# Query and key projections of one attention stage as two halves of 256 columns instead of one matmul of 512

## The chip, the cores and the metric

The kernel runs on one core of one Trainium2 chip. The metric is the device time of one execution in microseconds (us). Three runs of the kernel before gave 2101.59 us as their median, from 2100.45 to 2105.27.

## What is computed

Four blocks follow one another on an activation x of 16 batches x 128 rows x 256 features, with a context of the same shape: a channel attention (stage 0), a transformer layer with self and cross attention (stage 1), a latent attention (stage 2) and a block with two wide cross attentions and an MLP (stage 3). Only stage 3 is touched. Cut to what matters, in the reference it is

```python
D, H, K, F = (256, 16, 128, 1024)
def _cross_attention(q_in, kv_in, wq, bq, wk, bk, wv, bv, wo, bo, bias_k, bias_v):
    qh = (q_in @ wq + bq).reshape(b, q_len, H, K)
    kh = (kv_in @ wk + bk).reshape(b, t, H, K)
    vh = (kv_in @ wv + bv).reshape(b, t, H, K)
    kh = jnp.concatenate([kh, bias_k ...]); vh = jnp.concatenate([vh, bias_v ...])
    weights = softmax(einsum('bqhk,bthk->bhqt', qh, kh) / scale)
    return einsum('bhqt,bthk->bqhk', weights, vh).reshape(b, q_len, H * K) @ wo + bo
x = x + _cross_attention(_layer_norm(x, ...), xf_1, ...)
x = x + _cross_attention(_layer_norm(x, ...), xf_2, ...)
x = x + gelu(_layer_norm(x, ...) @ w_fc1 + b_fc1) @ w_fc2 + b_fc2
```

Both contexts are the same array. There are 16 heads of 128 columns, over 16 x 128 rows of x and of the context.

## The kernel before, in words

Stage 3 works through two attention layers (a = 0, 1), each as 8 pairs of heads. All rows, 16 batches x 128 = 2048, are cut in G = 4 quarters of R = 512 rows. A pair has STEPS = 8 steps, t = 0 to 7: one for each head and quarter. In every step TensorE (PE) makes, in this order: the scores of this step into a score bank (L1997, plain fp32, 8 recorded matmuls of 128 columns), the weighting of the values of the step before into o_psum (L2015, again 8), then the step's share of the projections and output products, and last the 4 transposes of the probabilities (L2074). The projections are one step or more ahead of their use; their order is the list in `pair_work` (L1204), and they go through four PSUM banks of 512 columns named `general`, taken in turn.

All products of projections and outputs use split numbers: each operand is held as a high part and a low part in the format fp32r, and `split_matmul` (L1949) adds three products (high x high, low x high, high x low) for each of the KC = 2 chunks of 128 features, thus six matmuls for each result. Each of the six has its own stationary operand, so that each matmul comes with one weight load.

- `queries` (L1972) and `keys` (L1978) fill one bank with one result of 128 rows x 512 columns: stationary is a 128x128 piece of w_qk, moving are 512 rows of hT (the normalised x, transposed) or of ctxT (the context, transposed). Six matmuls of 512 columns.
- `values` (L1983) and `output` (L2018) fill a bank with two results of 256 columns, one after the other: 12 matmuls of 256 columns. Stationary is ctxT or oT, moving is w_v or w_o.

In a whole pair there are 8 query and 8 key projections (96 matmuls of 512 columns), 8 banks of values and 8 of outputs (192 matmuls of 256 columns), 64 score matmuls, 64 for the weighting and 32 transposes. The pairs are: a `lead` pair written out, six pairs in a hardware loop (`pe.Fori(1, PAIRS - 1)`, L2139 and L2156), and a last one written out (`turn` after the first layer, `end` after the second). The lead pair has no values to make, since these were made before it.

The steps of a looped pair hold, after the 8 + 8 matmuls of scores and weighting: steps 1 and 2 two projections and two banks of values; step 3 one projection and two banks of values; step 4 three projections alone; steps 5 and 6 two projections and two banks of outputs; step 7 two projections and one bank of outputs. Step 0 has two projections and two banks of values right behind the last outputs of the pair before, which in the trace stand as a string of 24 matmuls of 256 columns, with the wait for the low part of oT inside it.

What runs beside: ScalarE (ACT) takes queries out of PSUM (L1622), makes the exponentials (L1629) and copies the transposed probabilities (L1637) and the weighted values (L1645); VectorE (DVE) takes out keys (L1768) and values, the maximum of the scores (L1782) and adds outputs to x (L1806); GpSimd (POOL) divides the probabilities by their sums (L1533) and subtracts high parts for low parts, of hT at L1502. Each general bank has a count `full` and a count `free`; a projection waits for `free` before its first matmul, and its last matmul raises `full`. `next_queries` (L2098) makes the queries of head 0 of a layer's first pair and waits for the low part of hT (`hT_ready`) inside the projection, ahead of the two matmuls that read it (`wait_low`, L1956).

Three key projections of the first pair are made in stage 2 by other code (L1160), and the MLP's up product has its own function (L2107).

Of the kernel before, what the change touches and what calls it, by code (L numbers as in the profile page):

```python
# [26 lines left out]
P = 128  # L27
B = 16
D = 256
KC = D // P  # L30
NB = 4
G = B // NB
R = NB * P
# [1292 lines left out]
def stage_3(nc, dram, consts, early):  # L1326

    ident, cols = consts["ident"], consts["cols"]

    with ExitStack() as ctx:  # L1330
        def sb(name, shape, dt=F32):
            return ctx.enter_context(nc.sbuf_tensor(name, shape, dt))
# [9 lines left out]
        rows = sb("rows3", [P, len(ROWS_B), D])  # L1342
# [12 lines left out]
        kT, ctxT, raw_qk, raw_v, raw_vrows = [early[name] for name in ("kT", "ctxT", "raw_qk", "raw_v", "raw_vrows")]  # L1355
        w_qk, w_v, vrow, hcols = [early[name] for name in ("w_qk", "w_v", "vrow", "hcols")]
        mv, rstd, shift = early["mv"], early["rstd"], early["shift"]
        hT = sb("hT3", [P, 2, KC, B * P], F32R)
# [40 lines left out]
        def wait_free(eng, *at):  # L1399

            k, n = bank_count(*at)
            eng.wait_ge(free[k], n + 1)
            return general[k], full[k]
# [26 lines left out]
        def quarter(g):  # L1430
            return slice(g * R, (g + 1) * R)
# [10 lines left out]
        with nc.Block() as block:  # L1442
# [503 lines left out]
            def _(pe):  # L1946
                seed(pe, [s["scores_ready"], s["pT_ready"], s["o_ready"]] + full)

                def split_matmul(out, stationary, moving, low_last=None, wait_low=None):  # L1949


                    terms = [(a, b, c) for c in range(KC) for a, b in PASSES]
                    if low_last is not None:
                        terms.sort(key=lambda term: term[low_last] == LO)
                    for i, (a, b, c) in enumerate(terms):
                        if wait_low is not None and i == 2 * KC:  # L1956
                            wait_low()
                        last = nc.tensor.matmul(out, stationary(a, c), moving(b, c), start=(i == 0), stop=(i == len(terms) - 1))  # L1958
                    return last

                def transposed(section, a, g):
                    for c in range(KC):
# [6 lines left out]
                            last = nc.tensor.transpose(out[:, b * P:(b + 1) * P], xhat(g, b)[:, c * P:(c + 1) * P], ident[:, :])  # L1969
                        last.then_inc(filled, 1)  # L1970

                def queries(section, a, i, key, head, wait_low=None):  # L1972
                    out, filled = wait_free(pe, section, a, i, key)
                    t = key[1]
                    split_matmul(out[:, :], lambda part, c: w_qk[:, head, part, c * P:(c + 1) * P],
                                 lambda part, c: hT[:, part, c, quarter(t % G)], 1, wait_low).then_inc(filled, 1)

                def keys(section, a, i, t, head):  # L1978
                    out, filled = wait_free(pe, section, a, i, ("k", t))
                    split_matmul(out[:, :], lambda part, c: w_qk[:, head, part, (KC + c) * P:(KC + c + 1) * P],  # L1980
                                 lambda part, c: ctxT[:, part, c, quarter(t % G)]).then_inc(filled, 1)

                def values(section, a, i, key):  # L1983

# [46 lines left out]
                def pair(a, i, kind):  # L2031
                    section, loop = kind, i if kind == "pair" else 0
                    weights = a * PAIRS + i + 2
                    for t in range(STEPS):
# [22 lines left out]
                        for key in pair_work(kind)[t]:  # L2057
                            if key[0] == "q":
                                queries(section, a, loop, key, 1 - key[1] // G)
                            elif key[0] == "late":  # L2060
                                next_queries(section, a, key)
                            elif key[0] == "k":
                                keys(section, a, loop, key[1], 1 - key[1] // G)
                            elif key[0] == "v":
                                values(section, a, loop, key)
                            else:
                                if key[2] == 0:
                                    pe.wait_ge(s["o_hi"], n + 1)
                                output(section, a, loop, key[1], key[2], (lambda: pe.wait_ge(s["o_lo"], n + 1)) if key[2] == 0 else None)
# [28 lines left out]
                def next_queries(section, a, key):  # L2098

                    pe.wait_ge(s["hT_hi"], a * G + key[1] % G + 2)  # L2100
                    queries(section, a, 0, key, 0, lambda: pe.wait_ge(s["hT_ready"], a * G + key[1] % G + 2))
# [18 lines left out]
                def down(g, f, b):  # L2120
                    if f == 0 and g > 0:
                        pe.wait_ge(s["down_added"], (g - 1) * NB + b + 1)
                    for k, (up_part, down_part) in enumerate(PASSES):
                        last = nc.tensor.matmul(down_sums[b][:, 0:D], upT[:, up_part, f, b * P:(b + 1) * P], w_down[:, down_part, f, :],  # L2124
                                                start=(f == 0 and k == 0), stop=(f == FC - 1 and k == len(PASSES) - 1))
                    return last

                keys("open", 0, 0, 7, 0)
                next_values("open", 2)
                transposed("open", 0, 0)  # L2130
# [36 lines left out]
                for g in range(G - 1):  # L2167

                    for f in range(FC):
                        up(g + 1, (f,))  # L2170
                        wait_upT(g, f)
                        for b in range(NB):
                            last = down(g, f, b)
                        last.then_inc(s["down_read"], 1)
                for b in range(NB):
                    for f in range(FC):
                        if b == 0:
                            wait_upT(G - 1, f)
                        last = down(G - 1, f, b)
# [103 lines left out]
```

## Time and profile before

| | |
|---|---|
| median of three runs | 2101.59 us (2100.45 to 2105.27) |
| profiled execution, its span | 2100.9 us |
| what lies around the span in the profiled execution | not shown on its own; the median of the runs is 0.7 us above the span |
| TensorE busy | 1933.4 us, 92% of the span |
| weight loads busy (overlap with the matmuls) | 1680.5 us |
| VectorE, ScalarE, GpSimd busy | 1277.2, 1184.1, 678.0 us |
| matmuls recorded | 14880, with as many weight loads |
| of them projections of queries and keys by `queries` and `keys` | 768 + 750, of 512 columns |
| stage 3 | from about 950 us to the end |

How to read it: a matmul's recorded duration holds the way through the array, so that it overlaps with the next one's. The pace of a row of matmuls is the time from the start of its first one to the start of what comes next, divided by their number, and not the duration of one. The timeline merges neighbours of one kind in one row, with the start of the first and the time until the end of the last.

### The profile page before, as it was taken

Reading aid. Unit: us, or ns where it says so; the run is one execution under the profiler, and the core shown is the slowest. Engines: PE = TensorE matmul, PEld = TensorE weight load, DVE = VectorE, ACT = ScalarE, POOL = GpSimd, SP = SyncE. Lnnn points to the kernel's source line nnn. Section 1 sums busy time; section 2 is a strip of 40 time slices with the busy share of each in tenths; the row PEclk is TensorE's granted clock in tenths of the full one; section 3 lists DMA queues with packets and bytes.
Section 4 is the critical chain, followed back from the end, with each engine's and each line's share of the span. In section 5 each row is a group of like instructions: output and inputs, shape, how many; then the busy total and the mean of one; then the engine's idle time right before and its main releaser. Section 6 shows DMA issues by size and latency. Waiting matters only on the chain.

```text
span 2100.9 us, 43190 instructions
## 1 busy us (share of the span) xinstructions
PE 1933.4 (92%) x14880; PEld 1680.5 (80%) x14880; DVE 1277.2 (61%) x4143; ACT 1184.1 (56%) x3878; POOL 678.0 (32%) x613
## 2 busy tenths in 40 slices
PE   4578899999999899888999999999899999999889
PEld 3457678787778777676999999999799999999778
DVE  2577797979797865445555555556455555555663
ACT  2466888778787876546444444443644444444531
POOL 1233443434444343533222221223312222223452
PEclk8889999999999999999999999999999999999999
DMA  7000000000000000001000000000000000000100
GB/s 262 6 11 7 6 7 7 12 2 7 2 7 2 3 2 2 22 1 43 26 16 25 25 20 15 25 15 26 11 26 21 20 25 20 15 20 0 41 11 31
DMA packets 24635, 44.35 MB, mean 21 GB/s; under 512 B 2336, under 2 KB 12064, under 8 KB 23584
## 3 DMA queue, kind: packets, MB, share of 16 engines
q1 hardware_dynamic: 23328, 34.13, 5.2%
q10 hardware_dynamic: 1152, 8.26, 1.0%
q8 instruction: 85, 1.39, 0.3%
q14 instruction: 70, 0.57, 0.1%
HBM read 40.28 MB, written 2.10 MB: 20 GB/s over the span
## 4 chain that ended last, share of the span: by engine, by line
PE 48%; DVE 2%; ACT 2%; issue 1%; POOL 1%; ACTq 0%; DVEq 0%; POOLq 0%
PE general L1958 32%; PE o_psum L2015 6%; PE scores L1997 5%; PE pT_psum L2074 3%; PE scores L2124 1%; ACT probs L1629 1%; POOL probs L1533 1%; PE o_psum L2124 1%; PE pT_psum L2124 1%; ACT oT L1645 0%; DVE oT L1800 0%; PE general L1969 0%; DVE guess L1310 0%; DVE var L1308 0%; DVE row_stats L1762 0%
## 5 line engine op out<-in xcount | busy, mean ns | idle before, releaser
L557 POOL TENSOR_TENSOR probs<-probs,rsums 128x512 f32<-128x512 f32 (+1 forms) x288 | 283.9, 998 | 485.8 <-DVE rsums L787 485.2
L1533 POOL TENSOR_TENSOR probs<-probs,rsums 128x512 f32<-128x512 f32 x128 | 133.4, 1042 | 733.0 <-DVE rsums L1793 733.0
L610 ACT ACTIVATE probs<-negated,negmax 128x128 f32<-128x128 f32 (+1 forms) x768 | 325.5, 431 | 12.1 <-DVE negmax L778 11.9
L1637 ACT COPY probsT<-pT_psum 128x512 f32<-128x512 f32 x128 | 75.0, 586 | 282.6 <-PE pT_psum L2074 282.6
L1105 PE MATMUL pT_psum<-ident,probs 128*128 128x128 f32 x1072 | 174.9, 284 | 53.9 <-ACT probsT L618 26.4
L1105 PEld LDWEIGHTS pT_psum<-ident,probs 128*128 128x128 f32 x1072 | 124.4, 144 | 108.2 <-issue 63.2
L1958 PE MATMUL general<-hT,w_qk 128*128 128x512 f32 x768 | 206.3, 404 | 1.9 <-ACT kT L1612 1.5
L1958 PE MATMUL general<-w_o,oT 128*128 128x256 f32 x1536 | 197.4, 282 | 1.6 <-ACT oT L1645 0.9
L1958 PE MATMUL general<-ctxT,w_qk 128*128 128x512 f32 x750 | 194.1, 394 | 2.9 <-DVEq L222 2.9
L1958 PEld LDWEIGHTS general<-w_o,oT 128*128 128x128 f32 x1536 | 187.8, 188 | 11.3 <-DVE oT L1800 3.8
L1629 ACT ACTIVATE probs<-scores,negmax 128x128 f32<-128x128 f32 x512 | 180.5, 370 | 24.0 <-DVE negmax L1785 24.0
L1645 ACT ACTIVATE oT<-o_psum,hcols 128x512 fp32r<-128x512 f32 x128 | 88.1, 688 | 183.5 <-PE o_psum L2015 183.5
L1958 PEld LDWEIGHTS general<-w_v,ctxT 128*128 128x128 f32 x1488 | 180.0, 189 | 4.5
L1958 PE MATMUL general<-w_v,ctxT 128*128 128x256 f32 x1488 | 182.1, 279 | 0.0
L1800 DVE SCALAR_TENSOR_TENSOR oT<-o_psum,hcols,oT 128x512 fp32r<-128x512 f32 x128 | 96.1, 751 | 119.1 <-ACT oT L1645 119.1
L1958 PEld LDWEIGHTS general<-ctxT,w_qk 128*128 128x128 f32 x750 | 139.4, 188 | 32.7 <-DVEq L222 3.3
L793 DVE COPY probsT<-pT_psum 128x512 f32<-128x512 f32 (+1 forms) x140 | 91.3, 652 | 116.6 <-PE pT_psum L1105 116.3
L1958 PEld LDWEIGHTS general<-hT,w_qk 128*128 128x128 f32 x768 | 136.2, 189 | 26.5 <-issue 2.1
L967 PE MATMUL general<-hT_y,weights_a 128*128 128x256 f32 x640 | 151.6, 383 | 2.6 <-ACT upT L683 1.5
L618 ACT COPY probsT<-pT_psum 128x512 f32<-128x512 f32 (+1 forms) x144 | 80.4, 558 | 126.7 <-PE pT_psum L1105 123.9
L610 ACT ACTIVATION_READ_ACCUMULATOR probs<-negated,negmax 128x1 f32 x768 | 148.7, 194 | 0.0
L2015 PE MATMUL o_psum<-probsT,ctxT 128*128 128x128 f32 x1024 | 141.4, 281 | 1.4 <-ACT probsT L1637 1.4
(198 smaller groups left out, 3922.7 us busy)
## 6 DMA issues: line engine op xcount, KB each, us to landing
raw_qk<-w_qk_dram SPq DMA_DIRECT2D x32, 256.0 KB, 2.8
weights_a<-weights_a_dram ACTq DMA_DIRECT2D x2, 2048.0 KB, 17.8
raw_v<-w_v_dram SPq DMA_DIRECT2D x16, 256.0 KB, 2.7
raw_vrows<-vrows_dram SPq DMA_DIRECT2D x16, 256.0 KB, 3.3
raw_o<-w_o_dram SPq DMA_DIRECT2D x16, 256.0 KB, 2.6
weights_a<-weights_a_dram ACTq DMA_DIRECT2D x3, 1024.0 KB, 10.4
X<-x_dram SPq DMA_DIRECT2D x8, 256.0 KB, 7.3
ctx_in<-ctx_dram SPq DMA_DIRECT2D x8, 256.0 KB, 2.8
```

What stands on the lines that cost most here:

```text
L557: nc.gpsimd.tensor_tensor(pr, pr, rsums[:, n % 4, 0:segs].unsqueeze(2).broadcast_to([P, segs, width(kind) // segs]), ALU.mult).then_inc(s[ ...
L610: last = nc.scalar.activation(probs[:, n % PROBS, i * wide:(i + 1) * wide], src[:, i * wide:(i + 1) * wide], ACT.Exp, scale=1.0 if kind == ...
L793: nc.vector.tensor_copy(probsT[:, n % 4, 0:width(kind)], turned(kind, g, u)[:, 0:width(kind)]).then_inc(s["pT_copied_dve"], 1)
L967: last = nc.tensor.matmul(out[:, j * RA:(j + 1) * RA], w[weight][:, c, chunk * P:(chunk + 1) * P], rhs(c), start=(c == 0), stop=(c == KC - 1))
L1105: last = nc.tensor.transpose(turned(kind, g, u)[:, j * P:(j + 1) * P], probs[:, n % PROBS, j * P:(j + 1) * P], ident[:, :])
L1533: nc.gpsimd.tensor_tensor(pr, pr, rsums[:, t % 2, :].unsqueeze(2).broadcast_to([P, NB, P]), ALU.mult).then_inc(s["probs_ready"], 1)
L1629: nc.scalar.activation(probs[:, t % 2, b * P:(b + 1) * P], scores[t % 2][:, b * P:(b + 1) * P], ACT.Exp, bias=negmax[:, t % 2, b:b + 1], s ...
L1645: nc.scalar.activation(oT[:, HI, head, quarter(t % G)], o_psum[:, :], ACT.Identity, bias=hcols[:, bass.ds(at, 1)]).then_inc(s["o_hi"], 1)
L1800: nc.vector.scalar_tensor_tensor(out=oT[:, LO, head, quarter(t % G)], in0=o_psum[:, :], scalar=hcols[:, bass.ds(at, 1)], in1=oT[:, HI, hea ...
L1958: last = nc.tensor.matmul(out, stationary(a, c), moving(b, c), start=(i == 0), stop=(i == len(terms) - 1))
L1997: last = nc.tensor.matmul(scores[t % 2][:, j * P:(j + 1) * P], qT[:, head, b * P:(b + 1) * P], kT[:, head, b * P:(b + 1) * P], start=True, ...
L2015: last = nc.tensor.matmul(o_psum[:, j * P:(j + 1) * P], v[:, head, (t % G) * NB + j, :], probsT[:, j * P:(j + 1) * P], start=True, stop=True)
```

## The change

`queries` and `keys` fill their bank in two halves: first all six matmuls on columns 0 to 255, then all six on columns 256 to 511. Each half loads its six stationary operands anew. Each result is the same sum in the same order. The count `full` is raised by the last matmul of the second half. The wait for the low part of hT stands in the first half, behind its first four matmuls.

```diff
+                def halves_matmul(out, stationary, moving, at, low_last=None, wait_low=None):
+                    for half in range(2):
+                        cols = slice(half * R // 2, (half + 1) * R // 2)
+                        rows = slice(at + half * R // 2, at + (half + 1) * R // 2)
+                        last = split_matmul(out[:, cols], stationary, lambda part, c: moving(part, c, rows), low_last, wait_low if half == 0 else None)
+                    return last
+
                 def queries(section, a, i, key, head, wait_low=None):
                     out, filled = wait_free(pe, section, a, i, key)
                     t = key[1]
-                    split_matmul(out[:, :], lambda part, c: w_qk[:, head, part, c * P:(c + 1) * P],
-                                 lambda part, c: hT[:, part, c, quarter(t % G)], 1, wait_low).then_inc(filled, 1)
+                    halves_matmul(out, lambda part, c: w_qk[:, head, part, c * P:(c + 1) * P],
+                                  lambda part, c, rows: hT[:, part, c, rows], t % G * R, 1, wait_low).then_inc(filled, 1)
 
                 def keys(section, a, i, t, head):
                     out, filled = wait_free(pe, section, a, i, ("k", t))
-                    split_matmul(out[:, :], lambda part, c: w_qk[:, head, part, (KC + c) * P:(KC + c + 1) * P],
-                                 lambda part, c: ctxT[:, part, c, quarter(t % G)]).then_inc(filled, 1)
+                    halves_matmul(out, lambda part, c: w_qk[:, head, part, (KC + c) * P:(KC + c + 1) * P],
+                                  lambda part, c, rows: ctxT[:, part, c, rows], t % G * R).then_inc(filled, 1)
```

## Rows read from the trace of the kernel before

**Rows 1.** The page, part 1: busy time, share of the span, instructions.

```profile
PE 1933.4 (92%) x14880; PEld 1680.5 (80%) x14880; DVE 1277.2 (61%) x4143; ACT 1184.1 (56%) x3878; POOL 678.0 (32%) x613
```

**Rows 2.** Stretches: length, busy PE, PEld, DVE, ACT, POOL, then PEclk; second: one pair.

```profile
1090.00:1404.00 314.00, 313.82 (x2236) 290.59 (x2235) 163.93 (x319) 145.77 (x500) 70.40 (x65) 1.00 0.07 21
...
1152.90:1215.87 62.97, 62.92 (x451) 58.24 (x450) 32.99 (x65) 29.15 (x100) 14.08 (x13) 1.00 0.07 21
```

**Rows 3.** Chain of waits from 1216 to 1280 us, by line.

```profile
by line: PE general L1958 70.5%; PE o_psum L2015 11.9%; PE scores L1997 9.8%; PE pT_psum L2074 5.5%; DVE oT L1800 1.2%; ACT oT L1645 1.1%; issue 0.3%; ACTq L1644 0.0%
```

**Rows 4.** The page, part 5: TensorE's groups of projections, values and outputs.

```profile
L1958 PE MATMUL general<-hT,w_qk 128*128 128x512 f32 x768 | 206.3, 404 | 1.9 <-ACT kT L1612 1.5
L1958 PE MATMUL general<-w_o,oT 128*128 128x256 f32 x1536 | 197.4, 282 | 1.6 <-ACT oT L1645 0.9
L1958 PE MATMUL general<-ctxT,w_qk 128*128 128x512 f32 x750 | 194.1, 394 | 2.9 <-DVEq L222 2.9
...
L1958 PE MATMUL general<-w_v,ctxT 128*128 128x256 f32 x1488 | 182.1, 279 | 0.0
```

**Rows 5.** Timeline of PE, steps 0, 4 and 5: start, us to last end.

```profile
1217.78 1.54 PE L1958 MATMUL general<-hT,w_qk 128*128 128x512 f32 x6
...
1220.53 2.91 PE L1958 MATMUL general<-w_v,ctxT 128*128 128x256 f32 x24
1223.28 0.60 PE L2074 MATMUL pT_psum<-ident,probs 128*128 128x128 f32 x4
...
1247.59 1.63 PE L1958 MATMUL general<-ctxT,w_qk 128*128 128x512 f32 x6
1249.06 1.54 PE L1958 MATMUL general<-hT,w_qk 128*128 128x512 f32 x6
...
1251.81 0.60 PE L2074 MATMUL pT_psum<-ident,probs 128*128 128x128 f32 x4
...
1254.01 1.62 PE L1958 MATMUL general<-hT,w_qk 128*128 128x512 f32 x6
...
1256.84 2.91 PE L1958 MATMUL general<-w_o,oT 128*128 128x256 f32 x24
1259.59 0.60 PE L2074 MATMUL pT_psum<-ident,probs 128*128 128x128 f32 x4
```

**Rows 6.** Timeline of PE, the 96 matmuls of 256 columns after the first layer.

```profile
1462.55 3.07 PE L1958 MATMUL general<-w_v,ctxT 128*128 128x256 f32 x24
1465.46 2.99 PE L1958 MATMUL general<-w_o,oT 128*128 128x256 f32 x24
1468.29 5.82 PE L1958 MATMUL general<-w_v,ctxT 128*128 128x256 f32 x48
```

**Rows 7.** Timeline of PE in the last pair; third row: the first's tail alone.

```profile
1942.51 2.98 PE L1958 MATMUL general<-w_v,ctxT 128*128 128x256 f32 x24
1945.33 1.54 PE L1958 MATMUL general<-ctxT,w_qk 128*128 128x512 f32 x6
...
1942.84 2.54 PE L1958 MATMUL general<-w_v,ctxT 128*128 128x256 f32 x21
```

**Rows 8.** Timeline of PE, two of the 14 output banks behind transposes.

```profile
1211.17 1.66 PE L1958 MATMUL general<-w_o,oT 128*128 128x256 f32 x12
...
1606.26 1.62 PE L1958 MATMUL general<-w_o,oT 128*128 128x256 f32 x12
```

**Rows 9.** Waits of PE over the whole span, its row for L2074.

```profile
PE pT_psum L2074 <- POOL probs L1533: 12.0, 10, 2.5
```

**Rows 10.** Timeline of PE, the first query projection and what follows.

```profile
959.86 0.73 PE L1958 MATMUL general<-hT,w_qk 128*128 128x512 f32 x2 [0.32 <-POOL hT L1502]
...
963.35 0.66 PE L1969 MATMUL general<-ident,xhat 128*128 128x128 f32 x4 [1.80 <-DVE ctxT L1775]
```

**Rows 11.** The page: the instruction queue (part 3), a load's landing (part 6).

```profile
q8 instruction: 85, 1.39, 0.3%
...
raw_o<-w_o_dram SPq DMA_DIRECT2D x16, 256.0 KB, 2.6
```

## The prediction

> **What bounds the kernel now.** First the page's busy times: PE is busy for 92% of the span [rows 1]. A share over the span says nothing of one stage, so next the stretches: in five pairs of the loop PE is busy for 313.82 of 314.00 us at the full clock of 2.4 GHz (granted 1.00), while VectorE has 163.93 us of work and ScalarE 145.77 [rows 2]. The chain of waits agrees: from 1216 to 1280 us 70.5% of it is L1958, where projections, values and outputs are multiplied, and nearly all the rest is PE as well [rows 3]. So what a change adds to PE's row of matmuls in the loops comes out in the time one for one, and the other engines' idle time takes nothing of it up.
>
> **What is cut.** 768 + 750 matmuls of 512 columns [rows 4] are 253 projections of six. They become 3036 of 256 columns, with as many weight loads: 1518 matmuls and 1518 loads more, 16398 recorded of each kind instead of 14880. No transfer, copy or count is added, and a bank is full when its second half is. So all hangs on whether two matmuls of 256 take longer than one of 512.
>
> **The tempting reading is wrong.** The groups give 400.4 us for 1518 matmuls of 512, 264 ns each, and 379.5 us for 3024 of 256, 125.5 ns each [rows 4]; two halves would take 251 ns and the change save 13 ns x 1518 = 20 us. But these busy times count the way through the array (394 ns recorded for a matmul of 512) once more at each change of group, and this is spread over 6 matmuls in a projection and over 12 or 24 in values. Starts are what counts. From 1249.06 to 1251.81 us 12 matmuls of 512 take 2.75 us, 229 ns each; from 1256.84 to 1259.59 us 24 of 256 take the same 2.75 us, 114.6 ns each, 229 ns for two [rows 5]. Here halving costs nothing: the price goes by columns, and the weight load of each half is hidden, as it already is in the values and outputs.
>
> The rows thus show no fixed part per matmul. The Trainium skill (TensorE: Matmul & The Clock Gate, "Back-to-back issue gap") has one, N / 2.4 + 2.5 ns: by that rule each of 1518 cut matmuls costs 2.5 ns more, and the sum would be about 4 us higher than at equal prices. The rows at 229 ns and 2 x 114.6 ns contradict it for these operands, and they decide.
>
> **But 256 columns have two paces.** In the string of 96 after the first layer 24 matmuls take 2.83 us (1465.46 to 1468.29 us), 118 ns each, and the 48 behind them keep to it: 5.82 less one duration of 0.28, by 47 gaps, is 118 ns [rows 6]. In the last pair 24 such matmuls take 2.82 us with their start, and the last 21 of them (2.54 - 0.28) / 20 = 113 ns each [rows 7]. Both are alone on PE, both begin right behind the weighting of values, both at full clock. A string keeps its pace to its end: the 96 never leave 118 ns. The 14 output banks that stand alone behind a transpose show how often each comes: 9 take 1.66 us and 5 take 1.62, which over ten gaps is the same 4 to 5 ns [rows 8]. Of the four undisturbed strings that begin with 256 columns behind the weighting, the one of rows 6 is slow and the three of the last pair (those at 1936, 1942 and 1949 us; [rows 7] is the second) are fast. Together 10 of 18 are slow.
>
> Before, a step behind the weighting begins with 512 columns; the values or outputs that follow come out at 2.75 us for 24 [rows 5], close to the fast pace. After, every step is one unbroken string of 256 columns from its first projection on. So the change makes the whole step, also its values and outputs, fall to the one or the other pace.
>
> **The sum, for one looped pair.** A string of n halves takes, slow, 2.91 us for its first 24 (1462.55 to 1465.46) and 0.118 for each more [rows 6]; fast, 2.82 for its first 24 and 0.113 for each more [rows 7].
> - Four steps (1, 2, 5, 6) have two projections and 24 matmuls of 256. Now 1254.01 to 1259.59 = 5.58 us [rows 5]. After, 48 halves: fast 2.82 + 2.71 = 5.53 (-0.05), slow 2.91 + 2.83 = 5.74 (+0.16).
> - Three steps (3, 4, 7) have the work of 36 halves; step 4 stands for them: 1247.59 to 1251.81 = 4.22 us [rows 5]. After: fast 2.82 + 1.36 = 4.18 (-0.04), slow 2.91 + 1.42 = 4.33 (+0.11).
> - Step 0 runs on behind the last outputs: 1217.78 to 1223.28 = 5.50 us [rows 5] for 48 halves' work. Fast 48 x 0.113 = 5.42 (-0.08), slow 48 x 0.118 = 5.66 (+0.16).
> All fast: -0.20 - 0.12 - 0.08 = -0.40 us a pair. All slow: +0.64 + 0.33 + 0.16 = +1.13.
>
> How many pairs: 253 / 16 = 15.8. Off the path are projections in steps where PE waits for the divided probabilities anyway: 10 such waits, 12.0 us together, at L2074 [rows 9], with two or three projections ahead of each, and the three before the first step. Some 27 go, 226 stay, 14 pairs. Bounds: 14 x -0.40 = **-5.6 us** and 14 x 1.13 = **+15.8 us**. I take half the strings at 118 ns, between the 10 of 18 over all and the 1 of 4 behind the weighting: +5.1 us.
>
> **Small things, at nothing.** The wait for hT's low part now stands behind four short matmuls instead of four long ones, with eight short ones (0.92 us) behind it instead of two long (0.46). It binds once, for 0.32 us at 959.86; the 0.46 us more are covered by the wait of 1.80 us that follows at 963.35 [rows 10]; without it they would count. Banks are filled at the same moments within 0.2 us, and the engines that empty them are half idle.
>
> Against the profiled span: 2100.9 + 5.1 = 2106.0 us. The median of the runs lies 0.7 above that span: **2107 us**.
>
> **The rivals.**
> 1. *Mixed paces*, the forecast: 35 to 80% of the strings at 118 ns, +2 to +11.5 us; chance 0.49.
> 2. *113 ns prevails* (the other side: not slower). If the start behind the weighting nearly always leads to 113 ns, as in three of four, the change takes out the slower beginning of the 512s and gives -5.6 to about +1 us, 2096 to 2103. It is decided by the share of strings at 118 ns: the time stays within 0.2% (4.2 us, about what a measurement tells from no change) below a share of (4.2 + 5.6) / 21.4 = 0.46, and is faster by over 0.2% only below 0.07. For it: rows 7. Against it: rows 6 and 8. Chance 0.27.
> 3. *Nearly all at 118 ns*, as the 96 in a row: +11.5 to +15.8, 2113 to 2117. Chance 0.14.
> 4. *The loop's code no longer stays on the core.* One pair has 451 matmuls and 450 loads in the trace [rows 2]. 29760 of both are recorded [rows 1], of which ten repeats of the loops are 9010; the other 20750 against 1.39 MB on the instruction queue are 67 bytes each [rows 11]. Were each repeat fetched again, the queue would carry about 2.0 MB. So a body of 60 KB is kept now; after, with 192 more, it is 73 KB. No row shows whether that much is kept. If not, each of ten jumps back waits for a fetch; the nearest row is a load that lands after 2.6 us [rows 11]: up to 26 us, 2127 with equal paces, or nothing if PE's queue covers it. Chance 0.06. The Trainium skill (Runtime: NRT & Kernel Launch, "Instruction fetch mechanics") gives PE 128 KiB, which would hold 73 KB, but says as well that a jump back beyond two blocks of 16 KiB stalls; the second is not what the 1.39 MB show, since the body is nearly four such blocks already.
> 5. *The busy times were right*: 13 ns saved each, -17 us on 14 pairs, 2084. Only the group means speak for it; the starts speak against. Chance 0.04.
> That the change does not do what it says would show in the count; the diff leaves no case out.
>
> **How the numbers follow.** Faster by over 0.2%: all of 5 and a fifth of 2, 0.09. Slower by over 0.2%: two thirds of 1, all of 3 and 4, 0.53. Within: 0.38. The range runs from nearly all fast, 2097, to all slow, 2117, and leaves out 4, 5 and the edge of 2. The likeliest case's own range is 2104 to 2113.
>
> **What would show it.** 16398 matmuls and loads, none of 512 columns in the projections; PE still busy all through the loops at 1.00; strings of 36 and 48 halves at 4.18 or 4.33 and 5.53 or 5.74 us, in about equal numbers; one looped pair of 63.3 to 63.6 us instead of 62.97 [rows 2]. The forecast is wrong if nearly all strings have one pace, if a third pace appears (the first halves of a bank above 118 ns would be loads that are not hidden), if gaps appear at the loop's ends, or if the instruction queue carries far more than 1.39 MB and the 0.07 MB of new code.

## The result and the profile after

Over 16 runs of each, the changed kernel takes 2109.1 us in the median (2106.85 to 2117.46) and the kernel before 2103.51 us (2099.47 to 2110.7). The ratio is 1.003, with a 95% interval of 1.002 to 1.0039: slower by 5.6 us or 0.27%, with an interval clear of 1. The profiled execution has a span of 2107.1 us against 2100.9.

The page after, span, busy times and TensorE's groups; they answer to [rows 1] and [rows 4]:

```profile
span 2107.1 us, 46226 instructions
PE 1942.2 (92%) x16398; PEld 1757.1 (83%) x16398; DVE 1277.1 (61%) x4143; ACT 1182.9 (56%) x3878; POOL 677.3 (32%) x613
...
q8 instruction: 89, 1.46, 0.3%
...
L1958 PE MATMUL general<-hT,w_qk 128*128 128x256 f32 x1536 | 208.8, 284 | 2.3 <-ACT kT L1612 1.5
L1958 PE MATMUL general<-ctxT,w_qk 128*128 128x256 f32 x1500 | 197.1, 280 | 2.9 <-DVEq L222 2.9
L1958 PE MATMUL general<-w_o,oT 128*128 128x256 f32 x1536 | 197.8, 282 | 1.7 <-ACT oT L1645 0.9
...
L1958 PE MATMUL general<-w_v,ctxT 128*128 128x256 f32 x1488 | 183.6, 280 | 0.0
```

The counts are the forecast ones: 16398 matmuls and as many loads, none of 512 columns in these groups. The other engines' work is unchanged. The four groups' busy times together grow from 779.9 to 787.3 us, +7.4; the values, which the change does not touch, have 1.5 of that. The instruction queue carries 89 packets instead of 85.

Where the 6.2 us of the spans lie. The stages ahead of the change vary from one execution to the next: the first query projection starts at 958.47 us in the profile before and at 957.35 after, 1.1 us earlier. So stage 3, from there to the end, takes 2107.1 - 957.35 = 1149.75 us instead of 2100.9 - 958.47 = 1142.43, which is 7.3 us more. The timeline of PE at the start of stage 3, after, answers to [rows 10]:

```profile
957.35 0.62 PE L1958 MATMUL general<-hT,w_qk 128*128 128x256 f32 x4
958.75 1.21 PE L1958 MATMUL general<-hT,w_qk 128*128 128x256 f32 x8 [0.78 <-POOL hT L1502]
...
962.26 0.66 PE L1969 MATMUL general<-ident,xhat 128*128 128x128 f32 x4 [1.82 <-DVE ctxT L1775]
```

The wait for the low part of hT is 0.78 us instead of 0.32, since four short matmuls now stand ahead of it. The wait of 1.8 us behind the next transposes is still there. From the first query projection to the transposes behind that wait it is 4.91 us (957.35 to 962.26), and it was 4.88 (958.47 to 963.35).

The loops, by stretches (length, then busy PE, PEld, DVE, ACT, POOL, then the granted clock), after; the first and second row answer to [rows 2]:

```profile
1090.00:1404.00 314.00, 313.79 (x2693) 311.61 (x2692) 162.73 (x317) 144.83 (x499) 70.26 (x65) 1.00 0.07 21
1153.40:1216.98 63.58, 63.53 (x547) 63.02 (x546) 32.94 (x65) 29.10 (x100) 14.06 (x13) 1.00 0.07 21
1216.98:1280.60 63.62, 63.57 (x547) 63.05 (x546) 33.03 (x65) 29.10 (x100) 14.05 (x13) 1.00 0.06 21
```

PE has no gap and the full clock, as before, and a pair takes 63.6 us instead of 63.0. From one jump back to the next the ten looped pairs took 62.97 to 63.09 us in the first layer and 63.26 to 63.44 in the second before, and 63.49 to 63.62 and 63.79 to 63.95 after: 0.6 us more for a pair in each layer, 5.9 us over the ten. Lead and last pairs and the start of the stage give the other 1.4.

Inside a pair, the timeline of PE after, steps with 48 halves (first and second) and one with 36 (third); they answer to [rows 5]:

```profile
1163.03 1.66 PE L1958 MATMUL general<-hT,w_qk 128*128 128x256 f32 x12
1164.53 1.58 PE L1958 MATMUL general<-ctxT,w_qk 128*128 128x256 f32 x12
1165.94 2.90 PE L1958 MATMUL general<-w_v,ctxT 128*128 128x256 f32 x24
1168.68 0.60 PE L2083 MATMUL pT_psum<-ident,probs 128*128 128x128 f32 x4
...
1170.87 1.66 PE L1958 MATMUL general<-hT,w_qk 128*128 128x256 f32 x12
1172.37 1.57 PE L1958 MATMUL general<-ctxT,w_qk 128*128 128x256 f32 x12
1173.78 2.99 PE L1958 MATMUL general<-w_v,ctxT 128*128 128x256 f32 x24
1176.60 0.60 PE L2083 MATMUL pT_psum<-ident,probs 128*128 128x128 f32 x4
...
1185.38 1.66 PE L1958 MATMUL general<-ctxT,w_qk 128*128 128x256 f32 x12
1186.87 1.58 PE L1958 MATMUL general<-hT,w_qk 128*128 128x256 f32 x12
1188.29 1.58 PE L1958 MATMUL general<-ctxT,w_qk 128*128 128x256 f32 x12
1189.70 0.60 PE L2083 MATMUL pT_psum<-ident,probs 128*128 128x128 f32 x4
```

Read the starts. In both of the first two steps the keys take 1.41 us for 12, 118 ns each, so the projections are at the slow pace. Then the steps part: the values of the first take 2.74 us for 24 (114 ns each), those of the second 2.82 (117.5). The steps take 5.65 and 5.73 us, where 5.58 stood before. The step of 36 halves is at the slow pace to its end, 4.32 us instead of 4.22.

For a count over the whole of stage 3, all gaps between neighbouring starts in unbroken rows of matmuls of 256 columns at L1958 (950 to 2000 us) were sorted to the nearer pace; a bank's row is called by the pace of most of its gaps. The counts of rows below use it. Before, 899 matmuls of 256 columns are slow and 1978 fast; after, 3672 and 2079. So 2773 more are slow, at 4.5 ns each +12.5 us; 1518 matmuls of 512 columns, at 229.8 ns in the mean, are gone, and two halves at 113.3 ns would be 3.2 ns quicker than one of these, -4.9 us. The sum, +7.6, is near the +7.3 us of stage 3, so the paces account for the cost. By place, each matmul counted from its start to the next one's: the projections take 4.9 us more, the values and outputs 2.1 and everything else 0.3.

### The profile page after: what moved, and what is told of

Read it like the earlier page. It is cut to its first block, busy times and chain, and to the rows that moved or that the text cites. A ratio compares the mean times of both kernels' runs of the same rounds, so it can differ in the third digit from the quotient of the medians.

```text
span 2107.1 us, 46226 instructions
## 1 busy us (share of the span) xinstructions
PE 1942.2 (92%) x16398; PEld 1757.1 (83%) x16398; DVE 1277.1 (61%) x4143; ACT 1182.9 (56%) x3878; POOL 677.3 (32%) x613
## 4 chain that ended last, share of the span: by engine, by line
PE 48%; DVE 2%; ACT 2%; issue 1%; POOL 1%; ACTq 0%; DVEq 0%; POOLq 0%
PE general L1958 32%; PE o_psum L2024 6%; PE scores L2006 5%; PE pT_psum L2083 3%; PE scores L2133 1%; ACT probs L1629 1%; POOL probs L1533 1%; PE o_psum L2133 1%; PE pT_psum L2133 1%; DVE oT L1800 1%; ACT oT L1645 0%; PE general L1969 0%; DVE guess L1310 0%; DVE row_stats L1762 0%; DVE totals L1791 0%
## 5 line engine op out<-in xcount | busy, mean ns | idle before, releaser
L1637 ACT COPY probsT<-pT_psum 128x512 f32<-128x512 f32 x128 | 74.9, 585 | 291.0 <-PE pT_psum L2083 291.0
L1958 PE MATMUL general<-hT,w_qk 128*128 128x256 f32 x1536 | 208.8, 284 | 2.3 <-ACT kT L1612 1.5
L1958 PE MATMUL general<-ctxT,w_qk 128*128 128x256 f32 x1500 | 197.1, 280 | 2.9 <-DVEq L222 2.9
L1958 PE MATMUL general<-w_o,oT 128*128 128x256 f32 x1536 | 197.8, 282 | 1.7 <-ACT oT L1645 0.9
L1958 PEld LDWEIGHTS general<-hT,w_qk 128*128 128x128 f32 x1536 | 188.6, 188 | 3.1 <-issue 2.1
L1958 PEld LDWEIGHTS general<-w_o,oT 128*128 128x128 f32 x1536 | 184.8, 188 | 7.3 <-DVE oT L1800 3.8
L1958 PEld LDWEIGHTS general<-ctxT,w_qk 128*128 128x128 f32 x1500 | 184.1, 188 | 3.3 <-DVEq L222 3.3
L1958 PE MATMUL general<-w_v,ctxT 128*128 128x256 f32 x1488 | 183.6, 280 | 0.0
L1958 PEld LDWEIGHTS general<-w_v,ctxT 128*128 128x128 f32 x1488 | 177.5, 189 | 0.0
```

## The experiments

Four theories stood against each other at different times. The *pace* theory: a row of 256 columns runs at 113 or 118 ns, set where it begins, whatever the number of matmuls. The *fixed price*: each further matmul costs some 2 to 3 ns. The *load floor*: the next load cannot finish sooner than some time behind the start of the matmul ahead, so that parts shorter than that show their loads. The *tie*: the slow pace comes about because a load of 128 columns takes nearly as long as 256 columns of streaming.

All times below are medians, each beside the kernel before on the same chip in the same batch. "Stage 3" is the profiled execution's time from the first query projection to the end, less that of the kernel before (1142.43 us).

### One kind of projection alone

```diff
 def queries(...):                              # e1: keys in halves, queries whole
-    halves_matmul(out, ..., t % G * R, 1, wait_low).then_inc(filled, 1)
+    split_matmul(out[:, :], ..., 1, wait_low).then_inc(filled, 1)
```
```diff
 def keys(...):                                 # e2: queries in halves, keys whole
-    halves_matmul(out, ..., t % G * R).then_inc(filled, 1)
+    split_matmul(out[:, :], ...).then_inc(filled, 1)
```

Keys in halves alone:

> Only key projections in halves, queries at 512. Pace theory (the price is which of two paces, 113 or 118 ns, a string of matmuls of 256 takes; a string that begins with a halved projection behind the weighting begins slow, one that begins with 512 columns falls to the fast pace at its first 256): steps begin with a query of 512, so keys, values and outputs behind it are fast; the looped pair stays within 0.15 us of 62.97, the whole within -3 to +2 us of before. Fixed-price theory (each added matmul and its load costs about 4 ns wherever it stands): 750 added, +3 us, looped pair 63.2.

Measured: 2105.62 us (11 runs) beside 2104.0, ratio 1.0014 [1.0004, 1.0023]; stage 3 +3.5 us. The timeline of PE with keys alone in halves, one step:

```profile
1170.41 1.63 PE L1958 MATMUL general<-hT,w_qk 128*128 128x512 f32 x6
1171.88 1.58 PE L1958 MATMUL general<-ctxT,w_qk 128*128 128x256 f32 x12
1173.30 2.90 PE L1958 MATMUL general<-w_v,ctxT 128*128 128x256 f32 x24
1176.03 0.60 PE L2083 MATMUL pT_psum<-ident,probs 128*128 128x128 f32 x4
```

The keys behind queries of 512 take 1.42 us, 118 ns each. In 69 of 105 rows of keys it is so, in 36 they are at 113 ns. That they would be fast behind 512 columns was wrong.

Queries in halves alone:

> Only query projections in halves, keys at 512. Pace theory: nearly every string begins with a halved query at 118 ns, the keys of 512 behind it go at 233 ns instead of 229, and the values or outputs behind those fall back to 113; about +0.05 us a string, looped pair 63.2 to 63.5, whole +3 to +7 us, clearly more than with the keys halved. Fixed-price theory: 768 added, +3 us, the same as with the keys halved.

Measured: 2105.69 us (11 runs), ratio 1.0016 [1.0006, 1.0025]; stage 3 +2.7 us. Of 90 rows of queries right behind the weighting of values, 85 are slow. Counted by place as above, the projections cost 2.1 us more with the keys in halves and 2.0 with the queries. Half the change costs about half of it, either half, so the two totals alone fit a fixed price for each further matmul as well as they fit the paces.

### The order of a step

```diff
-first = [[*head_1[0], *values[0]], [*head_1[1], *values[1]], ...
+first = [[*values[0], *head_1[0]], [*values[1], *head_1[1]], ...
```

The same for the last pair of the first layer; once on the changed kernel (e3), once on the kernel before (e8).

> Both halved as in the change, but in steps 0 to 3 of the looped and turn pairs the values stand ahead of the projections. Pace theory: strings that begin with values begin fast (4 of 4 in the changed kernel) and keep it, so in steps 1 to 3 the 24 + 24 or 24 + 12 take 5.53 and 4.18 us; 0.3 to 0.4 us less a looped pair than 63.57, 4 to 5 us less than the changed kernel, about the time of before. Fixed-price theory: the number of matmuls is the same, so the time is that of the changed kernel, +6 us.

> The kernel before (projections at 512) with the values ahead of the projections in steps 0 to 3, as in the run that had both. If that run's extra 9 us over the change are waits from the order (246 ns ahead of the weighting, 1 us more per looped pair in the scores), they appear here alone: 2108 to 2113 us. If they come from the halves, this stays at 2101.

Measured: in halves 2117.98 us (6 runs, two of them near 2111 and four near 2118), ratio 1.0055 [1.0041, 1.007], the looped pairs of the first layer 64.15 to 64.75 us; whole 2111.09 us (one run) beside 2106.82 (one run), stage 3 +10.4, pairs 63.61 to 64.10. In both kernels the new order costs more than the old one. The timeline of PE, values first, in halves:

```profile
1165.40 1.06 PE L2006 MATMUL scores<-kT,qT 128*128 128x128 f32 x8
1166.43 1.13 PE L2024 MATMUL o_psum<-probsT,ctxT 128*128 128x128 f32 x8
1167.32 3.07 PE L1958 MATMUL general<-w_v,ctxT 128*128 128x256 f32 x24
1170.22 1.58 PE L1958 MATMUL general<-hT,w_qk 128*128 128x256 f32 x12
1171.64 1.58 PE L1958 MATMUL general<-ctxT,w_qk 128*128 128x256 f32 x12
```

Two things come out. The values at the head of a step are now slow (2.90 us for 24, with their start) in 34 of 43 rows, where they stood behind the weighting as the three fast strings did on which rival 2 was built [rows 7]. And the scores take 1.03 us to the start of the weighting instead of 0.89: with the projections later in the step, the weighting waits for its copy (13 waits for the copied probabilities of L1637 from 1000 to 1990 us instead of 2). The second is there in the kernel before as well: from the last score's start to the weighting's, stage 3 takes 6.3 us more in halves and 6.5 in matmuls of 512. As for the first, with projections of 512 the values at the head are fast in 27 of 43 rows, and the four rows of values that stand at a head in the changed kernel without a new order, three in the last pair and the first of the string of [rows 6], are fast in both of its profiles. So values at the head can be slow and are not bound to be, and neither order is a way out.

### The two halves in turn, and the products in another order

```diff
-for half in range(2):
-    last = split_matmul(out[:, cols], stationary, ...)
+for i, (a, b, c) in enumerate(terms):          # e4
+    for half in range(2):
+        last = nc.tensor.matmul(out[:, cols], stationary(a, c), moving(b, c, rows),
+                                start=(i == 0 and half == 0), stop=(i == len(terms) - 1 and half == 1))
```
```diff
 def keys(...):                                 # e11: high parts first in keys too
-    halves_matmul(out, ..., t % G * R)
+    halves_matmul(out, ..., t % G * R, 1)
```

> Both halved, but the two halves alternate, so that two matmuls in a row have the same stationary operand, loaded twice. Pace theory: the string begins with the same kind of matmul as in the change, so the time is within 3 us of the changed kernel, with mostly slow beginnings. Fixed-price theory: +6 us as well. If what costs is fetching a new stationary operand from memory, every second load is of the address just read, and half of the loss goes, +3 us.

> The change with the keys' six products in the queries' order (both chunks' products with the high part of ctxT first, those with its low part last). Same matmuls, loads and columns. Pace theory: strings begin with queries as before and mostly at 118 ns; only what follows the keys can change, within 3 us of the change, 2106 to 2112. Fixed-price theory: exactly as the change, 2109.

Measured: in turn 2108.97 us (11 runs) beside 2104.0, ratio 1.0026 [1.0017, 1.0036], stage 3 +6.0; the other order of products 2109.11 us (6 runs) beside 2102.0, ratio 1.0037 [1.0024, 1.005], stage 3 +6.2. Both are as the change, and so are their paces: 87 of 90 and 89 of 90 rows of queries behind the weighting are slow. A stationary operand loaded twice in a row costs no less than two different ones, and the order of the products plays no part in the time.

### Smaller and unequal parts

```diff
-for half in range(2):
+for half in range(4):                          # e5: four of 128 columns
...
+for start, end in ((0, 384), (384, R)):        # e6
+for start, end in ((0, 288), (288, R)):        # e7
```

> Projections in quarters of 128 columns: 24 matmuls and 24 loads each. If a load is hidden only while it is shorter than the matmul ahead of it, 128 columns go at the 112 ns of the score matmuls, 4 x 112 instead of 230 ns: 218 ns x 1356 = 296 us more, about 2397 us. If loads are hidden without limit, 4 x 57 ns, and the time is that of the change, 2105 to 2110. The body of the loop grows to about 99 KB; if it is kept on the core, the instruction queue has about 98 packets instead of 89, if not, over 150, with gaps at the loop's ends.

> Parts of 384 and 128 columns instead of 256 and 256, with the same number of matmuls and loads. If the price goes by columns and paces alone: 2105 to 2110 us, as the change. If a load needs 107 to 112 ns behind the start of the matmul ahead, 384 take 170 ns and 128 take 112: 282 ns instead of 230, 52 x 1356 = 70 us more, about 2171 us.

> Parts of 288 and 224 columns. 256 columns (107 ns at the full clock) are as long as a load seems to be, so the two paces could come from this tie. If a load's 112 ns are the floor: 127 + 112 = 239 ns instead of 230, +12 us, 2113 us, and a single pace in the 224 parts. If the two paces have nothing to do with the tie, both stay at 1.00 and 1.04 times the columns, and the time is 2105 to 2110 us.

Measured, one run each beside 2106.82: 2431.55, 2174.39 and 2119.38 us. The timelines of PE, quarters:

```profile
1173.59 2.88 PE L1958 MATMUL general<-ctxT,w_qk 128*128 128x128 f32 x24
1176.30 2.84 PE L1958 MATMUL general<-hT,w_qk 128*128 128x128 f32 x24
1178.98 2.85 PE L1958 MATMUL general<-ctxT,w_qk 128*128 128x128 f32 x24
1181.66 0.52 PE L2083 MATMUL pT_psum<-ident,probs 128*128 128x128 f32 x3
```

384 and 128 columns (a row of the timeline names the first shape and counts both):

```profile
1176.58 1.91 PE L1958 MATMUL general<-hT,w_qk 128*128 128x384 f32 x12
1178.33 1.87 PE L1958 MATMUL general<-ctxT,w_qk 128*128 128x384 f32 x12
1180.03 2.94 PE L1958 MATMUL general<-w_v,ctxT 128*128 128x256 f32 x24
```

A projection in quarters takes 2.68 us for 24, 112 ns each, where halves take 113 or 118 ns for twice the columns. Below some length the price is that of the load, 112 ns. The 384/128 split shows the same number in another way: 1.70 us for six of each is 283 ns for a pair, against 229 for one of 512. Its parts of 384 follow at about 173 ns, next to 3/4 of 229 = 172, but the first of a projection takes some 222. Its parts of 128 follow at 109 to 115 ns, but for the first behind those of 384: that one takes 58 ns, a quarter of 229, in all 253 projections. That fits a load for the matmul behind it which was done during the 384 columns ahead; the loads of the parts of 128 in a row start 108 to 112 ns apart in the trace. The estimate 229 + (112 - 57) = 284 comes out for a pair, since the quick first part of 128 and the slow first of 384 about balance. A looped pair takes 68.08 us, +5.1 over 96 projection matmuls, 53 ns each. At 288/224 a pair takes 64.20 us, 12.8 ns a matmul, where the floor alone would give about 12; the total is some 6 us above the 2113 expected, but 5 of these the kernel before has in this batch too. The total of the quarters, +325 us, is above the forecast of about +296. The forecast left out the 27 projections beside the waits for probabilities; in quarters they outgrow these waits, of which none is left (12.0 us before).

The quarters settle the loop's code too. Their page's instruction queue, and the stretch in the first loop:

```profile
q8 instruction: 98, 1.61, 0.3%
```
```profile
1090.00:1404.00 314.00, 313.79 (x2752) 311.87 (x2752) 122.43 (x237) 110.80 (x375) 54.03 (x50) 1.00 0.05 15
```

The body of a loop now holds 451 + 450 + 2 x 288 = 1477 matmuls and loads, some 99 KB at the prediction's 67 bytes. The queue brings 1.61 MB, 0.22 more than before: of the 9108 matmuls and loads added, 5760 lie in the ten repeats, and the other 3348 at 67 bytes are these 0.22 MB. Were the body fetched anew at each of the ten jumps back, the queue would carry some 1.0 MB more than it does. PE stays busy for 313.79 of 314 us.

### Shorter loads

```diff
-last = nc.tensor.matmul(out, stationary(a, c), moving(b, c), ...)
+m = P // 2 if short and 0 < i < len(terms) - 1 else P
+last = nc.tensor.matmul(out[0:m, :], stationary(a, c)[:, 0:m], moving(b, c), ...)
```

`short` is set in the projections of queries and keys: once on the changed kernel (e9), once on the kernel before (e10). The middle four of the six products then leave out their share of result rows 64 to 127.

> The change, but the middle four of each six matmuls of a half load and use only 64 of the 128 stationary columns (their share of rows 64 to 127 of the result is left out); the columns that stream through stay 256. Tie theory (the slow pace comes from a load of 128 stationary columns, 112 ns at the least, being as long as 256 moving columns, 113 ns): with loads of about half the length these four go at 113 ns whatever the string's state, 226 x 8 halves of which 70% now lose 4.5 ns, -5.6 us and perhaps the neighbours' too, 2101 to 2104 us. If the pace has nothing to do with the load's length: 2107 to 2111, as the change.

> The kernel before with the same four short loads of six in its projections at 512. Tie theory: its loads (112 of 230 ns) are far from the tie, so at most the 3 ns of spread above 226.7 goes, 0 to -3 us: 2100 to 2104. If short loads save anything by themselves (fewer stationary columns to read), it shows here as well, as much as in the run with halves.

Measured, in halves: 2110.58 us (6 runs) beside 2102.0, ratio 1.0043 [1.0029, 1.0058], stage 3 +6.2. Groups of weight loads in the first loop, then the timeline of PE:

```profile
L1959 PEld LDWEIGHTS general<-hT,w_qk 128*64 128x64 f32 x320 | 38.8, 134 | 0.0
...
L1959 PEld LDWEIGHTS general<-hT,w_qk 128*128 128x128 f32 x160 | 27.3, 188 | 0.0
```
```profile
1162.57 1.65 PE L1959 MATMUL general<-hT,w_qk 128*128 128x256 f32 x12
1164.06 1.57 PE L1959 MATMUL general<-ctxT,w_qk 128*128 128x256 f32 x12
1165.47 2.99 PE L1959 MATMUL general<-w_v,ctxT 128*128 128x256 f32 x24
```

Two of three loads are shorter by 54 ns (134 for 188), and the keys still take 1.41 us for 12. The tie theory falls: with that much room these loads no longer only just fit, and the pace is the same.

Measured, in matmuls of 512: 2105.77 us (12 runs), ratio 1.0022 [1.0013, 1.0031]; stage 3 +5.8. It was expected to be no slower than before, and it is slower. The timeline of PE, then the groups of the page:

```profile
1170.78 1.62 PE L1959 MATMUL general<-hT,w_qk 128*128 128x512 f32 x6
1172.24 1.54 PE L1959 MATMUL general<-ctxT,w_qk 128*128 128x512 f32 x6
1173.62 2.99 PE L1959 MATMUL general<-w_v,ctxT 128*128 128x256 f32 x24
1176.45 0.60 PE L2075 MATMUL pT_psum<-ident,probs 128*128 128x128 f32 x4
```
```profile
PE 1936.7 (92%) x14880; PEld 1629.5 (77%) x14880; DVE 1276.7 (61%) x4143; ACT 1182.7 (56%) x3878; POOL 677.4 (32%) x613
...
L1959 PE MATMUL general<-w_v,ctxT 128*128 128x256 f32 x1488 | 185.0, 281 | 0.0
```

Not one matmul or load is added (14880 of each), the projections' pace is that of before (230 ns), and yet 3.8 us are lost. By place, the projections take 1.5 us less than before, the values and outputs 4.9 more and everything else 2.4 more. The values behind the projections, untouched, now take 2.83 us for 24, in 51 of 52 rows at the slow pace where none of 53 was before, and their group is busy for 185.0 us instead of 182.1. Of 256-column matmuls 1919 are slow and 970 fast, where 899 and 1978 were. A price for each further matmul cannot make this loss; a pace that is set at the border between two kinds of work can. That such a border sets it is read from the rows; no run shows how.

### The change once more

> The change itself once more, for one more profile. If the pace of a string is set by what stands in the program around it, the same strings are slow again: 89 of 90 that begin with queries behind the weighting, and about the same looped pairs of 63.5 to 63.6 and 63.8 to 63.95 us. If it is chance in each execution, the share at the values and outputs (50 of 102 slow in the first profile) and the pairs differ by some tenths of a us. Time 2107 to 2111 us in both cases.

Measured: 2108.96 us (8 runs) beside 2104.29, ratio 1.0025 [1.0012, 1.0038]; span 2108.7, stage 3 +5.4. It is the same kernel, on the chip a second time with another profiled execution. How the paces stand, by place, in rows at 113 / 118 ns:

| | queries behind the weighting | values | outputs |
|---|---|---|---|
| before (queries of 512) | - | 53 / 2 | 43 / 5 |
| change, first profile | 1 / 89 | 28 / 27 | 24 / 24 |
| change, second profile | 3 / 87 | 39 / 16 | 43 / 5 |

Queries at the head of a step are slow in both, 176 of 180 rows. Keys at the head, in step 4 of a looped pair and its like, are less bound: 14 and 15 of 18 are slow. Nor are the values and outputs: of 138 rows of these, in all places, 42 changed from slow to fast from one profile to the other and 14 the other way, and stage 3 went from +7.3 to +5.4. So one profile's pace of a given row is not a property of the program, except for queries at the head.

What does return is the projections' own price. Counted by place they cost 4.9 us more than before in the first profile and 5.3 in the second, and 5.0, 5.3 and 4.3 with the halves in turn, with the keys' products in the other order and with shorter loads: about 3 ns for each matmul cut. The values and outputs add 2.1 us in the first profile and 0.5 in the second.

## Why the prediction was right

The forecast was +5.1 us on the profiled execution's 2100.9 and 2107 us in the median, within 2097 to 2117, slower by over 0.2% the likeliest. Measured: +6.2 us in the spans, +5.6 us in the medians of 16 runs each. The 2109.1 us lie another 2 us above the forecast because the kernel before has 2103.5 us over 16 runs, not the 2101.6 of its first three. Point by point:

- **What bounds it.** Right. PE has no gap in the loops after either, and what its four groups gained, +7.4 us, is close to what stage 3 gained.
- **The count.** Right: 16398 matmuls and loads.
- **The tempting reading.** Rightly refused. The halves' means are 284 and 280 ns, 564 and more for two, beside 404 and 394 for one of 512: a mean busy time mixes in the way through the array, and says neither -20 us nor, read the other way, +250 us. The starts decide.
- **Price by columns, loads hidden.** Right for 256 columns, and barely: the parts of 128 and 224 columns show that the load sets the price, 112 ns, as soon as the parts in a row are shorter than about 256 columns. The prediction named a third pace above 118 ns as the sign of bare loads; the halves have none.
- **Two paces.** Right, in both numbers: 1.41 us for 12 keys is 118 ns, 2.74 us for 24 values is 114. A slow step of 48 halves was forecast at 5.74 us and takes 5.73, a slow one of 36 at 4.33 and takes 4.32.
- **Half the strings slow.** Undersized. By its own scale (-0.40 us a pair all fast, +1.13 all slow) the looped pairs' +0.59 in the first profile mean a share of (0.59 + 0.40) / 1.53 = 65%, and the +0.43 of the second 54%. 14 pairs x 0.59 would be +8.3 us; stage 3 shows 7.3. Queries at the head of a step are slow in 176 of 180 rows, not by a toss, and the keys behind them with them; the values and outputs vary, and are slow in less than half of the rows over both profiles. That +5.1 came so near is in part luck: the half was taken between two samples of rows without a query, and what the queries have above it is partly offset by what the values and outputs have below. The three fast rows of the last pair [rows 7], on which rival 2 stood, are fast again after the change, but they were no sample of the queries that now stand at the head.
- **A string keeps its pace to its end.** Wrong where it passes from projections to values or outputs. Behind slow keys these take either pace, as in the first and second step shown above. Behind the rarer fast keys the values were slow in each of 13 rows in the first profile, and in 20 of 20 with keys alone in halves. From one projection to the next the pace stays: 103 of 103 from queries to keys, 17 of 17 from keys to queries. The 96 matmuls in a row of [rows 6], which gave the rule, keep to one pace in the first profile after as well, but to the other one: 24 in 2.82 us with their start, 24 in 2.72 us, and the last 48 in 5.60 us, less 0.28 by 47 gaps 113 ns. So the rule holds among values and outputs, and which pace it is was no property of the string.
- **Small things.** Right in the sum. The wait for hT's low part is 0.78 us, +0.46, and all but 0.03 us is covered behind it (4.91 us instead of 4.88). The wait named as the cover, 1.80 us, has not shrunk (1.82); what went is the wait of 0.34 us ahead of the first four transposes.
- **Rival 4, the loop's code.** Refuted. 0.07 MB more on the queue, no gap at a loop's end, and a body of some 99 KB is kept too. The Trainium skill (Runtime: NRT & Kernel Launch, "Instruction fetch mechanics") has 128 KiB for PE. The 99 KB agree with that, though no run goes beyond it; its stall for jumps back beyond two blocks of 16 KiB shows in no run here.
- **Rival 5, busy times.** Refuted by the total.

The prediction weighed a rule of the Trainium skill (TensorE: Matmul & The Clock Gate, "Back-to-back issue gap"), N / 2.4 + 2.5 ns. By that rule the sum would have been about +3.8 us, or 3.4 on the 226 projections of the path, an estimate from its 2.5 ns. The measured 5.6 is not far from it, and so is what the projections alone cost, 4.9 and 5.3 us for the whole change and 2.1 and 2.0 for either half of it. The rows within contradict it: by that rule a matmul of 256 columns would follow at 109.2 ns, and they follow at 113.3 or 117.8, so the fixed part would have two sizes, 6.6 and 11.1; two halves at the fast pace take 226.6 ns, less than one of 512 with 229.8; and e10 lost 3.8 us with no matmul more. The rule of the Trainium skill came near by its total, not by its mechanism.

**What stays open** is what sets the pace. It is not the length of the loads (e9), nor a stationary operand being loaded twice (e4), nor the order of the products (e11), nor the number of matmuls (e10). It follows the borders between kinds of work: queries in halves behind the 128-column plain fp32 weighting are nearly always slow, keys there mostly, values there slow in 34 of 43 rows in e3 and fast in 4 of 4 in each profile of the change; borders from projections to values and outputs go either way, and borders between projections never change it. Why is not shown by any run here. Nor did any version beat the kernel before, which stays the fastest.

## What to carry to other kernels

Cutting a matmul in half was not free here, even with columns setting the price and each load hidden: look in the trace at the starts of the shorter form where it already stands, find every pace that it has, and price the change with the worst as well as the best. Do not cut below the length at which a load is still hidden, here about 256 columns: parts in a row below it cost the load's time, not their own. And of two profiles of one kernel, compare from the first instruction that the change touches; here the stages ahead differed by more than 1 us, a fifth of the effect.

## What the runs showed of the hardware that was not expected

- A row of fp32r matmuls of 256 columns, with one load of 128 columns each, has two steady paces at a granted clock of 1.00: 113.3 and 117.8 ns. One of 512 columns goes at 228.2 to 234.0 ns in the mean of a projection, 229.8 over all in the kernel before.
- At 128 columns each matmul with its load takes 112 ns, so the load of 128 columns is the floor, nearly twice the 57 ns of its columns. The floor holds for loads in a row: one matmul of 128 columns behind matmuls of 384 takes 58 ns. Loads with 64 columns are recorded 54 ns shorter, with nothing gained where they are hidden.
- Shortening loads in one kind of matmul slowed another kind behind it: 2.83 us for 24 values instead of 2.75.
- Pace at a border can differ between two executions of the same program: 42 of 138 rows of values and outputs went from 118 to 113 ns and 14 the other way, and stage 3 took 1149.7 and 1147.8 us.
- The program ahead of stage 3 ended anywhere from 955.3 to 962.0 us over the 14 profiles, with the same code there.
